# Local layers: the inverse norms of queries and keys by logarithm, exponential and a Newton step, in place of GpSimd's power

## The reference, cut to what matters

```
def l2norm(t):
    return t / jnp.maximum(jnp.linalg.norm(t, axis=-1, keepdims=True), 1e-12)
...
qkv = x @ Wqkv
q, k, v = jnp.split(qkv, 3, -1)
q = l2norm(q) * qs
k = l2norm(k) * ksc
q = q * cos * scale + rotate_half(q) * sin * scale
k = k * cos * inv + rotate_half(k) * sin * inv
out = local_attention(q, k, v)          # softmax over two windows of 32
return out.transpose(0, 2, 1, 3).reshape(b, n, INNER) @ Wo
...
for i in range(DEPTH):                  # 6
    x = attn_layer(shift_tokens(x), Wqkv[i], q_scale[i], k_scale[i], Wo[i]) + x
    x = ffn_layer(shift_tokens(x), ln_g[i], ln_b[i], W1[i], b1[i], W2[i], b2[i]) + x
```

## Time and profile before

| | |
|---|---|
| Median of 3 runs | 5192.28 us |
| Fastest and slowest | 5189.11 and 5200.19 us |
| Span of the profiled execution, first to last instruction | 5189.2 us |
| TensorE, VectorE, ScalarE, GpSimd busy | 93%, 74%, 63%, 66% |
| Local stage, by the turns of `b_qk` | 1161.9 to 4358.7 us |

### The profile page before, as it was taken

How to read it: one execution, slowest core, us unless ns; L and a number is a source line. 1 busy time by engine, 2 the same in 40 slices (tenths; PEclk the granted TensorE clock), 3 DMA queues, 4 the chain that set the end, 5 groups by cost and what they waited for, 6 DMA issues and landing times. The chain is left out here.

```text
span 5189.2 us, 207179 instructions
## 1 busy us (share of the span) xinstructions
PE 4824.2 (93%) x84978; PEld 3974.8 (77%) x84978; DVE 3833.9 (74%) x7791; ACT 3275.6 (63%) x6212; POOL 3434.7 (66%) x2250
## 2 busy tenths in 40 slices
PE   6999999989999999999999999999999997788879
PEld 4888888877888788878887788778887886555557
DVE  4777777768888788878887788788877885555543
ACT  2333333337777777767777777777777775566654
POOL 1221222229999999999999999999999995222212
PEclk8999999999999999999999999999999998898988
DMA  1000000013222322232223222332223222000000
GB/s 45 8 8 8 8 8 8 8 38 84 70 69 68 87 69 69 69 86 71 69 69 87 69 68 69 73 85 69 69 72 73 68 69 49 1 0 0 0 1 17
DMA packets 422079, 254.04 MB, mean 49 GB/s; under 512 B 201104, under 2 KB 418734, under 8 KB 420799
## 3 DMA queue, kind: packets, MB, share of 16 engines
q1 hardware_dynamic: 415008, 234.97, 19.1%
q10 hardware_dynamic: 6688, 13.45, 0.8%
HBM read 25.08 MB, written 4.25 MB: 6 GB/s over the span
## 5 line engine op out<-in xcount | busy, mean ns | idle before, releaser
L1311 POOL TENSOR_TENSOR b_rnorm<-b_ss,neghalf 128x16 f32<-128x16 f32 x384 | 1118.4, 2912 | 25.2 <-DVE b_ss L1847 20.8
L1307 POOL TENSOR_TENSOR b_rot<-b_t 128x1024 f32<-128x1024 f32 x384 | 909.6, 2369 | 75.0 <-DVE b_t L1836 74.8
L1834 DVE TENSOR_TENSOR b_t<-psum,b_cosg 128x1024 f32<-128x1024 f32 x384 | 469.6, 1223 | 424.8 <-ACT b_sq L1689 418.8
L1318 POOL TENSOR_TENSOR b_qk<-b_rot,b_rnorm 128x1024 f32<-128x1024 f32 x384 | 730.9, 1903 | 42.2 <-POOL b_rnorm L1311 0.9
L1435 PE MATMUL psum<-b_w_hi,b_xT_parts 128*128 128x512 f32 x1152 | 528.4, 459 | 26.9 <-issue 17.8
L1689 ACT ACTIVATE b_sq<-psum 128x1024 f32<-128x1024 f32 x384 | 391.7, 1020 | 223.4 <-PE psum L1440 223.0
L475 POOL TENSOR_TENSOR a_k_diag<-a_k_parts,a_head_rows 128x1024 fp32r<-128x1024 f32 x64 | 119.8, 1894 | 570.9 <-PE psum L622 531.6
L1841 DVE TENSOR_REDUCE b_ss_floor<-b_sq 128x16 f32<-128x1024 f32 x384 | 464.4, 1209 | 0.0
L1440 PE MATMUL psum<-b_w_hi,b_xT_parts 128*128 128x512 f32 x1152 | 460.4, 400 | 0.0
L1436 PE MATMUL psum<-b_w_lo,b_xT_parts 128*128 128x512 f32 x1152 | 457.7, 397 | 0.6 <-issue 0.6
L1522 PE MATMUL psum<-shared,b_oT 128*128 128x128 f32 x3072 | 425.3, 281 | 0.8 <-ACT b_oT L1707 0.8
(11 more groups left out here) (269 smaller groups left out, 11971.9 us busy)
## 6 DMA issues: line engine op xcount, KB each, us to landing
b_v_win<-b_v SPq DMA_DIRECT2D x2304, 65.0 KB
b_v_win<-b_v SPq DMA_DIRECT2D x1152, 32.5 KB
oa<-XR SPq DMA_DIRECT2D x1024, 2.0 KB
xcur<-X SPq DMA_DIRECT2D x111, 128.0 KB, 4.3
shared<-in_L_ffn_Wqkv_dram ACTq DMA_DIRECT2D x6, 1536.0 KB
b_x_shifted<-X SPq DMA_DIRECT2D x96, 64.0 KB
b_x_shifted<-X SPq DMA_DIRECT2D x96, 63.5 KB
shared<-in_L_ffn_Wo_dram SPq DMA_DIRECT2D x10, 256.0 KB, 3.2
```

The lines of the kernel that those rows point to most:

```text
L1307: nc.gpsimd.tensor_tensor(rot[:, i, :, :], t1[:, i, :, :], t2[:, i, :, :], ALU.add).then_inc(rot_done, 1)
L1311: nc.gpsimd.tensor_tensor(rnorm[:, i, :], ss[:, i, :], neghalf[:, :], ALU.pow).then_inc(rn_done, 1)
L1318: nc.gpsimd.tensor_tensor(qk[:, i, :, :], rot[:, i, :, :], rnorm[:, i, :, None].broadcast_to((P, 16, BD)), ALU.mult).then_inc(qk_done, 1)
L1834: nc.vector.tensor_tensor(t14, x4, tab(cosg, slice(0, BD), BD), ALU.mult)
```

## The change

GpSimd's power goes. ScalarE takes the logarithm of the floored sum of squares and then the exponential of minus half of it, a first guess g of the inverse norm. VectorE makes one Newton step of it in three operations: s·g, then -(s·g)·g, then (that + 3)·g, which is twice the inverse norm; the rotation's tables are halved on the host for that. ScalarE's two stand behind the exponentials in each slot, for block j+3, VectorE's three behind `normalise` and ahead of `residual`, for block j+3. The table set that holds logarithm and exponential is loaded by name, at the stage's start and once a sequence in slot 3. Three semaphores of the first layer's set-up become one that counts.

```
-    c["rot_cos"] = lay(cos * scale * f(8), cos * inv)
-    c["rot_sin"] = lay(sin * scale * f(8), sin * inv)
+    c["rot_cos"] = lay(cos * scale * f(4), cos * inv * f(0.5))
+    c["rot_sin"] = lay(sin * scale * f(4), sin * inv * f(0.5))
...
-            ev_turned, pp_turned = sem("a_ev_turned"), sem("a_pp_turned")
-            pp_full, set_ok = sem("a_pp_full"), sem("a_set_ok")
+            setup_full, set_ok = sem("a_setup_full"), sem("a_set_ok")
+            PP_PRODUCT, EV_TURNED, PP_TURNED = 1, 2, 3
...
                     def normalise_rows(n, s, deviations_of=None):
...
-                        pool.wait_ge(floor_done, m)
-                        nc.gpsimd.tensor_tensor(rnorm[:, i, :], ss[:, i, :], neghalf[:, :],
-                                                ALU.pow).then_inc(rn_done, 1)
...
+                    def guess_norms(s, m):
+
+                        i = s % 2
+                        act.wait_ge(floor_done, m)
+                        nc.scalar.activation(log_ss[:, i, :], ss[:, i, :], ACT.Ln).then_inc(guess_done, 1)
+                        act.wait_ge(guess_done, 2 * m - 1)
+                        nc.scalar.activation(rn_guess[:, i, :], log_ss[:, i, :], ACT.Exp, scale=-0.5).then_inc(guess_done, 1)
...
+                            if j == 3 and ffn:
+                                nc.scalar.preload_act_table_set(LOG_EXP)
                             if ok(j + 1):
                                 exps(j + 1, m + 1)
+                            if ok(j + 3):
+                                guess_norms(j + 3, m + 3)
...
+                    nc.scalar.preload_act_table_set(LOG_EXP)
                     one_pass("first", 0, 0, ffn=False)
...
+                    def improve_norms(s, m):
+                        i = s % 2
+                        dve.wait_ge(guess_done, 2 * m)
+                        nc.vector.tensor_tensor(rn_step[:, i, :], ss[:, i, :], rn_guess[:, i, :], ALU.mult).then_inc(step_done, 1)
+                        dve.wait_ge(step_done, 2 * m - 1)
+                        nc.vector.scalar_tensor_tensor(rn_step[:, i, :], rn_step[:, i, :], -1.0, rn_guess[:, i, :],
+                                                       ALU.mult, ALU.mult).then_inc(step_done, 1)
+                        dve.wait_ge(step_done, 2 * m)
+                        nc.vector.scalar_tensor_tensor(rnorm[:, i, :], rn_step[:, i, :], 3.0, rn_guess[:, i, :],
+                                                       ALU.add, ALU.mult).then_inc(rn_done, 1)
...
                             if ok(j + 1):
                                 normalise(m + 1)
+                            if ok(j + 3):
+                                improve_norms(j + 3, m + 3)
                             if ok(j):
                                 residual(b, j, m)
```

More of the change, by code:

```diff
@@ L397, in _ @@
                     nc.vector.tensor_tensor(ext[:, 3, :], ext[:, 0, :], ext[:, 2, :], ALU.mult).then_inc(made, 1)
-                    dve.wait_ge(pp_full, 1)
+                    dve.wait_ge(setup_full, PP_PRODUCT)
                     nc.vector.tensor_copy(pprow[0:1, 0:NREX], bank[0][0:1, 0:NREX]).then_inc(made, 1)
@@ L403, in _ @@
                         nc.vector.tensor_copy(part[:, :, :].rearrange("p a c -> p (a c)"), sum_in[:, t, :])
-                    dve.wait_ge(ev_turned, 1)
+                    dve.wait_ge(setup_full, EV_TURNED)
                     windows = psum[:, 1:7, :].rearrange("p a c -> p (a c)").rearrange("p (u c) -> p u c", c=P)
@@ L410, in _ @@
                                               .rearrange("p u (x l d) -> p (u x) l d", x=2, d=HD)).then_inc(made, 1)
-                    dve.wait_ge(pp_turned, 1)
+                    dve.wait_ge(setup_full, PP_TURNED)
                     nc.vector.tensor_copy(pp_tab[:, :, :].rearrange("p t l -> p (t l)"), bank[7])
@@ L419, in _ @@
                     nc.tensor.matmul(bank[0][0:1, 0:NREX], ones[0:HD, 0:1], ext[:, 3, :],
-                                     start=True, stop=True).then_inc(pp_full, 1)
+                                     start=True, stop=True).then_inc(setup_full, 1)
                     pe.wait_ge(ld_c, 16 * 7)
@@ L426, in _ @@
                                                 start=True, stop=True)
-                    last.then_inc(ev_turned, 1)
+                    last.then_inc(setup_full, 1)
                     nc.tensor.matmul(bank[7], flip[:, :], pp_flip.rearrange("p t l -> p (t l)"),
-                                     start=True, stop=True).then_inc(pp_turned, 1)
+                                     start=True, stop=True).then_inc(setup_full, 1)
             rk = lambda lt: [("rk", lt, n) for n in range(8)]
@@ L1068, in build_program @@
             rnorm = sb(st, "b_rnorm", [P, 2, 16])
+            log_ss, rn_guess, rn_step = (sb(st, f"b_{n}", [P, 2, 16]) for n in ("log_ss", "rn_guess", "rn_step"))
             t1, t2 = sb(st, "b_t1", [P, 2, 16, BD]), sb(st, "b_t2", [P, 2, 16, BD])
@@ L1115, in build_program @@
             masked = sem("b_masked")
+            guess_done, step_done = sem("b_guess_done"), sem("b_step_done")
+            LOG_EXP = "natural_log_exp_and_others"
             N_WA, N_LN, N_W1, N_W2 = 3, 2, 5, 3
```

## The result

The changed kernel takes 6172.64 us, the median of 4 runs (6169.8 to 6179.35), against 5190.69 for 4 runs of the kernel before on the same chip: 1.190 times as long, 95% interval 1.189 to 1.192. Forecast were 6025 us and a range of 5890 to 6260.

A forecast was written before the change was run, and what follows sets the result against it. TensorE was taken to bound the local stage. The span of 5189 us, plus 827 for the chain, less 40 for `b_xn`, plus 2 for table loads gave 5978; with 45 for the clock 6023, stated as 6025 us, range 5890 to 6260.

The forecast's parts named there:

- the forecast's own bounds: Limits for the chain with few or no clock drops, 5915 to 6153 us; this forecast had a chance of 0.79.
- the rival with half clock in every slot: Local stage: same chain, with TensorE at 1.2 GHz behind each stall; 6248 us, chance 0.14.
- The chain's length: From TensorE's slot end through VectorE and GpSimd to the next turn: 8.92 us late a sequence, 827 us after `b_qTs`.
- the prediction's sum: Span before plus chain, less returned `b_xn` waits, plus table loads, without the clock: 5978 us.
- The last step of the sum: From the span of 6023 us to the time of 6025, the median of runs standing 3 above the span.
- What comes back: TensorE's waits for `b_xn`: 40 of 45.5 us return as GpSimd's backlog goes; the `b_qTs` wait, 0.26 us, vanishes.
- one slot in six, 45 us: Local stage: low clock on TensorE behind its idle gaps, taken in one slot of six, adding 45 us.
- 0.7 us a slot: TensorE's slowdown in a slot at low clock, from slower projection matmuls and what else slows; 267 us if all slots.
- two lone gaps: TensorE gaps before the change: 2.30 us with granted clock 1.00, 2.56 us followed by 0.79; used to size clock drops.
- my own mark for being right: Sign in the profile after: the stage's granted clock stays above 0.93, against near 0.8 for half clock in every slot.

The follow-up runs named there:

- the first experiment: The changed kernel with VectorE's Newton step at the start of its slot, not behind the outputs' products: 5199.23 us, ratio 1.0025 to the kernel before.
- the second: The kernel before, power kept, with GpSimd's product of block m waiting until VectorE has normalised block m-2: 5946.75 us, ratio 1.147.
- ScalarE alone: The kernel before, power kept, plus the change's logarithm, exponential and table loads on ScalarE, results unused: 5209.26 us, ratio 1.0047.
- the experiment with more work: The changed kernel with the six projection matmuls of queries and keys issued twice in each slot: 5971.49 us, ratio 1.151 to the kernel before.
- one place earlier: The changed kernel with VectorE's Newton step ahead of `normalise` in place of behind it: 5377.23 us, ratio 1.039 to the kernel before.
- two more operations: The changed kernel with two more dependent VectorE operations of 16 columns ahead of the norm: 6510.22 us, ratio 1.258 to the kernel before.

## Why the prediction was right, and which term was too small

The direction and the mechanism were right, and so was the stall without the clock, in part by two errors that cancel; the clock was sized at a fifth of what it is. The measured 6173 us lie inside the range, but above the forecast's own bounds (5915 to 6153): the range holds them only because it reached on to 6260 for the rival with half clock in every slot. That part of the hit is luck.

**The bound and the place.** That TensorE bounds the stage and that the norm's new place, behind VectorE's wait for the end of TensorE's slot, makes a chain from slot to slot: shown, by the waits of the profile after, by the first experiment (the place undone: 16 us of the loss left) and by the second (the dependence without the operations: 763 us). One thing the prediction left out: in the kernel before, the turn of block k waited already for `b_o` of block k-2, whose place in PSUM it writes to (`o_done` in `turn_qk`), and seldom had to stand idle for it (13 waits, 10.7 us in all). The change puts the Newton step and GpSimd's product between the two, 2.8 us with their starts.

**The chain's length.** Forecast were 8.92 us of lateness a sequence, 2.23 a slot; TensorE waits 2.24 us a slot. These are not quite the same thing: the forecast is how much later the turn comes, the wait is idle time of TensorE behind its six projections. The pieces are less exact than the sum: from the end of the outputs to the turn it takes 3.9 to 4.1 us, not 3.6 to 3.9, because GpSimd and TensorE nearly always start 0.14 us behind their input, where 0.08 and 0.05 were taken from one row each. Over the inner slots without a low clock, before and after, this stretch grew by 2.38 us (1.58 to 3.96), 0.15 more than forecast, and the rest of the slot, from the turn to the end of the outputs, shrank by 0.26 us (6.68 to 6.42), where the forecast had 0.07 for `b_qTs`. The two errors cancel, and that the sum fits to a hundredth is luck. The Newton step takes 0.58 us, 0.60 forecast. The slot without a low clock takes 10.38 us, 10.4 forecast, and the kernel without the clock's part 5971 us, where the prediction's sum stood at 5978. (The last step of the sum is off by one: 6023 and 3 are 6026, not 6025.)

**What comes back.** `b_xn` gave back 28 us, not 40: the longest wait, 7.6 us, stays, as it does in the first experiment. `b_qTs` gave back 19 of 25 us or so, as it vanishes under the stall. ScalarE alone costs 26 us, not 38: 33 us more for `b_qTs`, 0.35 in each of 94 slots where 0.4 was taken, less 11 for `b_xn`.

**The clock: the step that failed.** It was "one slot in six, 45 us", at "0.7 us a slot". Measured are 155 slots of 367 (0.42) at 1.36 us, 211 us by counting, 201 by the experiment with more work, and 198 by TensorE's longer busy time. Both factors were too small. The count was read from two lone gaps of the kernel before, the nearer of which had no drop, as if the length of one gap decided; the two slots above, behind 2.31 and 2.33 us, show that it doesn't. Two gaps were also a thin choice from that trace: the stage has nine gaps over 1.8 us, eight of 2.56 to 4.22 us (all waits for `b_xn`), each with half clock beside it, and the one of 2.30 without. In the kernel before such a gap is rare, in the changed one it comes in each slot. The price missed that the turn behind the gap slows too (1.06 to 1.71 us), and the FFN's matmuls where they come next (four of them 1.47 us at 2472.03, against 1.03 for the same four in the experiment with more work, at 2412.03). The rival with low clock behind every stall (6248) was nearer, 75 us off where the forecast was 148 off, though not for its own reason: it had every slot touched at 0.7 us, and measured are two slots of five at twice that. The granted clock of 0.94 passed my own mark for being right ("above 0.93"), which shows how weak a mark it was: half clock for 12% of the stage reads as 0.94, and costs 200 us.

**The rule on engines.** Where the Trainium skill ("GPSIMD Engine Reference", section on engine selection) puts elementwise work on VectorE, the trace still agrees as to the engine (0.17 us for each small operation, 2.91 for the power, which is not the same operation). Placed where nobody waits, and for three blocks of four, the move is 6 us faster, at the edge of what the runs tell apart; placed behind `normalise`, it loses 982.

## What to carry to other kernels

Before you move an operation to a faster engine, write down what stands ahead of it there and what that waits for: on an engine that works in program order an operation of 0.2 us inherits each wait ahead of it, and if the bounding engine raises that wait at the end of its turn and needs the result early in the next, the whole link is added to every turn. Time taken off an engine with 4.5 us to spare is worth next to nothing (here some 10 us for 1104), so look first at who waits for it. And where a change puts a regular gap into TensorE's work, price the granted clock with a large count of gaps, both ways, and not from one lone gap: here it added a quarter to the stall.

## What the runs showed of the hardware

**Work that nobody needs made the kernel faster.** 2304 more matmuls took 201 us off, since the clock stayed at its upper level and the matmuls lay in time that was lost anyway.

**The clock's price grows faster than the wait.** Six kernels of this case, by TensorE's mean wait for `b_qk` in a slot, with the slots of 367 that a stretch of half clock touches, and the time at half clock in the stage:

| Kernel | wait, us a slot | slots touched | half clock, us |
|---|---|---|---|
| before | 0.01 | 16 | 37 |
| one place earlier | 0.64 | 1 | 10 |
| more work for TensorE | 0.93 | 1 | 12 |
| power held | 1.43 | 70 | 209 |
| the change | 2.24 | 155 | 495 |
| two more operations | 2.65 | 241 | 866 |

The 37 us of the kernel before stand beside its eight long waits for `b_xn`, and the held product has such waits too, so the first column is not the only cause. Why a given slot is touched and its neighbour not stays open: the length of the gap ahead does not tell. Besides the pair of 2.31 and 2.33 us above, in the changed kernel the slots of the first place wait 2.12 us on average and 60 of 92 are touched, those of the second 2.36 us and 35 of 92. No run here varied anything else alone.

**An engine's start behind another's end** is 0.05 to 0.15 us, and not one number: GpSimd behind VectorE 0.14 us at 2404.17 and 0.15 at 2414.78, TensorE behind GpSimd 0.05 us at 2406.12 and 0.15 at 2416.83; over the inner slots of the changed kernel the median of both is 0.14. On a link that is passed 384 times each 0.1 us is 38 us.
